# Gated expert rows scattered by token and choice, with the last norm in the experts' block, on one Trainium2 core

## What is computed

```python
gate_logits = x @ gate_w + gate_b
topk_vals, topk_idx = jax.lax.top_k(gate_logits, K)          # K = 2 of E = 16
topk_w = jax.nn.softmax(topk_vals, axis=-1)
h = jax.nn.relu(jnp.einsum('bsh,ehf->bsef', x, w1) + b1)     # 256 -> 512
expert_out = jnp.einsum('bsef,efh->bseh', h, w2) + b2        # 512 -> 256
sel = jnp.take_along_axis(expert_out, topk_idx[:, :, :, None], axis=2)
moe = jnp.sum(topk_w[..., None] * sel, axis=2)
y = x + moe
(y - mu) / jnp.sqrt(var + EPS) * gamma + beta                # and added to the residual
```

## Time and profile before

| | us |
|---|---|
| median of three runs | 1938.15 |
| the profiled execution | 1941.34 |
| its span, first to last instruction | 1939.4 |

### The profile page before, as it was taken

One profiled execution on the slowest core, in us unless ns is written; L12 is line 12 of the kernel. 1 busy time (PEld: TensorE's weight loads), 2 busy tenths in 40 slices (PEclk: granted clock), 3 DMA queues, 4 the chain that ended last, 5 costly groups with the idle time before them and its releaser, 6 DMA issues. The chain is left out here.

```text
span 1939.4 us, 33213 instructions
## 1 busy us (share of the span) xinstructions
PE 1445.2 (75%) x7648; PEld 1164.5 (60%) x7649; DVE 969.4 (50%) x3112; ACT 463.1 (24%) x1295; POOL 994.3 (51%) x1125
## 2 busy tenths in 40 slices
PE   5499968787769887877878788664899999996000
PEld 4366636565657665665756666442799899886000
DVE  8766556552737452742745275368211222221787
ACT  0144432121112111211212112010344444443000
POOL 0200027777777777777777777720233233223775
PEclk9799987989788899888899879775899999998555
DMA  6000043333333333333333333344322333532443
GB/s 215 1 0 0 0 144 104 104 106 103 103 105 104 103 103 105 103 104 105 103 103 105 105 101 105 104 132 137 113 78 70 113 94 95 189 92 64 131 137 115
DMA packets 105690, 193.84 MB, mean 100 GB/s; under 512 B 19056, under 2 KB 68976, under 8 KB 105520
## 3 DMA queue, kind: packets, MB, share of 16 engines
q0 software_dynamic: 47520, 129.82, 23.9%
q1 hardware_dynamic: 58128, 63.58, 9.8%
HBM read 159.11 MB, written 34.21 MB: 100 GB/s over the span
## 5 line engine op out<-in xcount | busy, mean ns | idle before, releaser
L701 POOL DMA_INDIRECT ring<-table,staged x784 | 747.5, 953 | 242.8 <-issue 226.3
L976 PE MATMUL bank<-ring,hots 128*128 x1372 | 323.9, 391 | 53.0 <-SPq L690 52.7
L976 PEld LDWEIGHTS bank<-ring,hots 128*128 128x128 f32 x1372 | 264.6, 195 | 102.7 <-issue 66.9
L1427 PEld LDWEIGHTS bank<-xT,w 128*128 128x128 f32 x1696 | 208.9, 194 | 15.5 <-issue 10.3
L1427 PE MATMUL bank<-xT,w 128*128 128x128 f32 x1696 | 210.2, 278 | 8.7 <-issue 8.7
L976 PE MATMUL bank<-ring,late_hots 128*128 x388 | 141.8, 518 | 97.4 <-SPq L690 88.8
L1405 ACT ACTIVATE hT<-bank,b 128x128 f32<-128x128 f32 x424 | 155.6, 367 | 226.0 <-PE bank L1427 202.4
L1435 PE MATMUL bank<-w,hT 128*128 128x256 f32 x848 | 201.7, 381 | 1.5 <-DVE y L1468 1.4
L786 DVE TENSOR_SCALAR hots<-iota_t,edge_l 128x128 f32<-128x128 f32 x686 | 182.1, 362 | 1.8
L976 PEld LDWEIGHTS bank<-ring,late_hots 128*128 128x128 f32 x388 | 92.5, 252 | 138.9 <-issue 124.3
L1348 POOL COPY at_x<-list 128x1 int32 (+1 forms) x108 | 19.6, 181 | 287.4 <-DVE xin L1450 201.2
(11 more groups left out here) (256 smaller groups left out, 2028.9 us busy)
## 6 DMA issues: line engine op xcount, KB each, us to landing
w<-in_w SPq DMA_DIRECT2D x32, 512.0 KB, 5.2
lists_out<-y SPq DMA_DIRECT2D x106, 128.0 KB, 2.7
ring<-table,staged POOLq DMA_INDIRECT x784
x<-in_x SPq DMA_DIRECT2D x1, 6272.0 KB, 23.4
table<-xn SPq DMA_DIRECT2D x7, 896.0 KB, 4.4
rows<-xn SPq DMA_DIRECT2D x1, 6272.0 KB, 21.1
out<-out_c SPq DMA_DIRECT2D x7, 512.0 KB, 3.1
out<-out_c SPq DMA_DIRECT2D x7, 384.0 KB, 2.6
```

The source lines that it names most:

```text
L701: pool.indirect_dma_start(out=ring[:, j, :], out_offset=None, in_=a.table, in_offset=bass.IndirectOffsetOnAxis(ap=staged[:, half, col:col ...
L976: last = nc.tensor.matmul(agg, hot[:, k, :], two[:, k, :], start=False, stop=False)
L1427: last = nc.tensor.matmul(up_ps[fc], w1[:, slot, ch, fc * P:(fc + 1) * P], xT[:, ch, :], start=(ch == 0), stop=(ch == DC - 1))
```

## The change

- **route**: the list gets a second column. The one-hot matmuls now carry `2 * lane + 1 + choice` instead of the lane, so that each list entry says token and choice. VectorE decodes it: which token to fetch, and in which row of the new HBM tensor `spread` (token, choice) the result belongs; unused rows go to dummy rows behind. `m.which` says per row which of the two gates applies. SyncE writes `rows` with 258 columns: the 256 of `m.xn` and the two gates, as two DMAs, the second after a wait on the gates.
- **experts**: GpSimd fetches rows of 258 columns and, itself, scatters each block's result to `spread` by an indirect DMA; SyncE sends no results and no zeros. VectorE, in iteration b, first waits for the result, adds the bias into a buffer of its own, waits for that and for a free half of `y`, copies the scatter's row numbers, multiplies by the gate into `y`; then it runs `rows_in(b + 2)`, which now also picks the gate out of the fetched rows and copies the row numbers of a later fetch, and only this last copy counts up `copied`. TensorE waits for `biased_ok` instead of `y_ok` before it reuses the result bank.
- **last norm**: in the same block. SyncE loads both rows of each token from `spread` by plain DMAs of four tiles, TensorE adds `m.xn` and the two rows in PSUM by three matmuls with the identity, and VectorE takes statistics and the norm from there, one batch of four tiles behind; ScalarE gives a seed by Ln and Exp.
- The buffers of the first stages are freed before the experts, and `with_beta` uses scalar_tensor_tensor.

```diff
@@ route
+        lane2 = sb("lane2", [P, 2], F16)
...
             sp.dma_start(rows[:, :, 0:D], m.xn[:]).then_inc(rows_out, 16)
+            sp.wait_ge(gates_ok, 1)
+            sp.dma_start(rows[:, :, D:D + 2], m.share[:]).then_inc(rows_out, 16)
             sp.dma_start(e.b1[:], a.b1).then_inc(e.b1_in, 16)
...
+            sp.wait_ge(rows_out, 32)
...
-                    dve.tensor_scalar(ids[part][:, :, 0], hi_hot[part][:], m.const[:, C_LANE:C_LANE + 1], None, ALU.mult)
+                    dve.tensor_tensor(ids[part][:, :, 0], hi_hot[part][:],
+                                      lane2[:, None, None, :].broadcast_to([P, n, BLOCKS, 2]), ALU.mult)
...
-            c.add(dve.tensor_tensor(m.list[:, 0:BLOCKS], tokens[:], list_ps[:, 0:BLOCKS], ALU.add))
+            c.add(dve.tensor_tensor(tokens[:], tokens[:], list_ps[:, 0:BLOCKS], ALU.add))
+            c.wait()
+            c.add(dve.tensor_copy(spot[:], tokens[:]))
+            c.add(dve.tensor_scalar(unused[:], tokens[:], 0.0, dummy[:, 0:1], ALU.is_equal, ALU.mult))
+            c.add(dve.tensor_copy(m.list[:, BLOCKS:BLOCKS + 1, 1], dummy[:]))
+            c.wait()
+            c.add(dve.tensor_single_scalar(first_i[:], spot[:], 1, ALU.bitwise_and))
+            c.add(dve.tensor_scalar(spot[:], spot[:], 1.0, -1.0, ALU.max, ALU.add))
+            c.wait()
+            c.add(dve.tensor_copy(m.which[:, 0:BLOCKS, 0], first_i[:]))
+            c.add(dve.tensor_scalar(m.which[:, 0:BLOCKS, 1], first_i[:], -1.0, 1.0, ALU.mult, ALU.add))
+            c.add(dve.tensor_single_scalar(spot[:], spot[:], 1, ALU.arith_shift_right))
+            c.wait()
+            c.add(dve.tensor_copy(m.list[:, 0:BLOCKS, 0], spot[:]))
+            c.add(dve.tensor_tensor(m.list[:, 0:BLOCKS, 1], tokens[:], unused[:], ALU.add))
@@ experts, GpSimd
+            def sent(of, n):
+                pool.wait_ge(y_ok, of + 2)
+                if not isinstance(of, int) or of > 0:
+                    pool.wait_ge(y_out, of * 16)
+                    pool.sem_inc(y_free, 1)
+                settle(pool, m)
+                pool.indirect_dma_start(out=a.spread, in_=y[:, 1 - n, :], in_offset=None,
+                                        out_offset=bass.IndirectOffsetOnAxis(ap=to[:, 1 - n:2 - n], axis=0)).then_inc(y_out, 16)
...
+                    fetched(i * 2 + (n + 4), n)
+                    landed(i + (n + 2), 1 - n)
+                    sent(i * 2 + (n + 1), n)
+            pool.wait_ge(y_out, pairs * 32 + 16)
+            pool.sem_inc(spread_ok, 1)
@@ experts, SyncE
+                    end = of_list(sp, 1, i * SLOTS + slot)
+                    sp.wait_ge(y_ok, end + 1)
+                    e.load(sp, i * SLOTS + (slot + SLOTS), slot)
+            sp.wait_ge(spread_ok, 1)
+            last_norm.sync(sp)
@@ experts, VectorE
             def rows_in(b):
                 dve.wait_ge(got_ok, b + 1)
                 if not isinstance(b, int) or b > 0:
                     dve.wait_ge(xtr_ok, b)
                     settle(dve, m)
-                dve.tensor_copy(xin[:], got[:, bass.ds(b % 2, 1), :].rearrange("p a d -> p (a d)")).then_inc(copied, 1)
+                dve.tensor_tensor(pick[:, bass.ds(b % 2, 1), :], got[:, bass.ds(b % 2, 1), D:D + 2], m.which[:, bass.ds(b, 1), :],
+                                  ALU.mult).then_inc(pick_ok, 1)
+                dve.tensor_copy(xin[:], got[:, bass.ds(b % 2, 1), 0:D].rearrange("p a d -> p (a d)"))
+                dve.wait_ge(pick_ok, b + 1)
+                settle(dve, m)
+                dve.tensor_tensor(gate[:, bass.ds(b % 4, 1)], pick[:, bass.ds(b % 2, 1), 0:1].rearrange("p a k -> p (a k)"),
+                                  pick[:, bass.ds(b % 2, 1), 1:2].rearrange("p a k -> p (a k)"), ALU.add)
+                fetched(b + 2)
...
                     with dve.Fori(first, end) as b:
+                        dve.wait_ge(down_ok, b + 1)
+                        dve.tensor_tensor(biased[:], down_ps, b2[:, slot, :], ALU.add).then_inc(biased_ok, 1)
+                        dve.wait_ge(biased_ok, b + 2)
+                        dve.wait_ge(y_free, b + 2)
+                        settle(dve, m)
+                        sent_to(b)
+                        dve.tensor_scalar(y[:, bass.ds(b % 2, 1), :].rearrange("p a d -> p (a d)"), biased[:], gate[:, bass.ds(b % 4, 1)],
+                                          None, ALU.mult).then_inc(y_ok, 1)
                         rows_in(b + 2)
-                        dve.wait_ge(down_ok, b + 1)
-                        dve.wait_ge(y_out, b * 16 + 16)
-                        dve.tensor_tensor(y[:], down_ps, b2[:, slot, :], ALU.add).then_inc(y_ok, 1)
@@ last norm, TensorE
+            if t >= 8:
+                pe.wait_ge(self.z_read, t - 8 + 1)
+            nc.tensor.matmul(to, m.ident, tile(m.xn, t), start=True, stop=False)
+            if t % 4 == 0:
+                pe.wait_ge(self.back[t // 4], 16)
+            for k in range(2):
+                last = nc.tensor.matmul(to, m.ident, self.got[:, t % self.LOADED, k, :], start=False, stop=(k == 1))
@@ last norm, VectorE
+        for q in range(len(self.batches)):
+            spreads(q)
+            if q > 0:
+                normal(q - 1)
+        normal(len(self.batches) - 1)
```

More of the change, by code:

```diff
@@ L32 @@
 BLOCKS = 2 * NP // BLOCK + E
-AHEAD = 2
 BATCH = 28
@@ L104, in memory @@
     m.places = sb("places", [P, NT, 2], I32)
[L105 removed]
+    m.list = sb("list", [P, BLOCKS + 4, 2], I32)
     m.lists = sb("lists", [1, 2, E], I32)
[L107 to L109 removed]
+    m.which = sb("which", [P, BLOCKS + 4, 2])
     m.ident = m.const[:, C_ID:C_ID + P]
@@ L1182, in _ @@
             c.wait()
-            c.add(dve.tensor_tensor(m.share[:, :, 1], eg[:], m.share[:, :, 0], ALU.mult))
+            dve.tensor_tensor(m.share[:, :, 1], eg[:], m.share[:, :, 0], ALU.mult).then_inc(gates_ok, 1)
             dve.wait_ge(rank_ok, 1)
@@ new lines, in _, with fetched @@
+            pool.sem_inc(y_free, 3)
+            pairs = nc.s_assert_within(of_list(pool, 1, E - 1) // 2, E // 2, BLOCKS // 2,
+                                       skip_runtime_bounds_check_because="half of all blocks")
+            def fetched(b, n):
+                pool.wait_ge(copied, b + 1)
+                settle(pool, m)
+                pool.indirect_dma_start(out=got[:, n, :], out_offset=None, in_=a.rows,
+                                        in_offset=bass.IndirectOffsetOnAxis(ap=at[:, n:n + 1], axis=0)).then_inc(x_in[n], 16)
@@ L1363, in _ @@
+            pool.wait_ge(x_in[1], pairs * 16 + 32)
+            settle(pool, m)
         @block.sync
         def _(sp):
-            def sent(i, more):
-                bounds = bounds_of(sp, i)
+            with sp.Fori(0, E // SLOTS - 1) as i:
                 for slot in range(SLOTS):
-                    first, end = bounds[slot:slot + 2]
-                    with sp.Fori(first, end) as b:
-                        sp.wait_ge(y_ok, b + 2)
-                        sp.dma_start(rows_of(a.lists_out, b), y[:]).then_inc(y_out, 16)
-                        sp.sem_inc(filled, 16)
-                    if more:
-                        e.load(sp, i * SLOTS + (slot + SLOTS), slot)
@@ L1577, in _ @@
[L1577 to L1591 removed]
+        self.m, self.a = m, a
@@ new lines, in __init__ @@
+        self.LOADED, self.DONE = 16, 12
+        self.batches = [(t, min(t + 4, NT)) for t in range(0, NT, 4)]
+        self.got = sb("got", [P, self.LOADED, 2, D])
+        self.z = sb("z", [P, 4, D])
+        self.out = sb("out_c", [P, self.DONE, D])
+        self.st = sb("st_c", [P, 2, 4, 6])
+        self.mv = sb("mv_c", [P, 2, 4, 2])
+        self.var = sb("var_c", [P, 2, 4])
+        self.lnv = sb("lnv_c", [P, 2, 4])
+        self.seed = sb("seed_c", [P, 2, 4])
+        self.nt = sb("nt_c", [P, 4])
```

321 lines of the change are left out of this document (153 added, 168 removed).

## The result

The changed kernel takes 2003.6 us (median of 4 runs, 2003.14 to 2004.04) against 1938.63 us: a ratio of 1.034, 95% interval 1.032 to 1.036. It is slower, as forecast, but by 65 us where 32 were forecast; the executions of each kernel agree within 0.3%.

| stretch | before | after | difference | forecast |
|---|---|---|---|---|
| up to the first product of the experts | 1369.65 | 1371.91 | +2.3 | +3 |
| from there to the last bias add | 409.6 | 519.3 | +109.7 | +69 |
| last bias add to the end | 160.1 | 109.7 | -50.4 | -40 |

The account below looks back on a forecast made before the run. TensorE was taken to bound the experts' loop, while the last stretch, with TensorE idle, could be shortened. Route +3, loop +69 and end -40 gave +32, so 1970 us, with an 8 in 10 range of 1918 to 2030.

Parts of the forecast that it names:

- The part named as the one that counts: Experts' loop: VectorE's work from the bias add to `copied` outlasts the 1.37 us TensorE leaves; +69 us.
- Route: Route: lane product as tensor_tensor, some seven more dependent steps, small memsets and copies, all on VectorE; +3 us.
- The gate pieces: Route: SyncE's 6272 writes of 8 bytes, priced from nothing to 21.1 us, costed at nothing for the first product.
- I take 0.65 us, nearer to the middle: Experts' loop: the TensorE stall chosen per block, with register instructions partly under work; 106 blocks, +69 us.
- middle case: Experts' loop: register instructions run beside the work in front; chain 1.82 us, stall 0.45 us a block, 48 us.
- upper case: Experts' loop: thirteen register instructions and five waits, none hidden after the bias; chain 2.54 us, stall 1.17, 124 us.
- lower case: Experts' loop: register instructions cost nothing, wait behind the bias 0.19; chain 1.63 us, stall about 0.28 a block, 30 us.
- The second term, the last stretch: Last bias add to the end: first norm at 28 us, cycles of 8.0, 120.6 us against 160.1; -40 us.
- a clock of 0.9: Last norm: TensorE's assumed granted clock, which makes the cycle of four tiles 8.0 us instead of 7.4.
- The hidden stall: Rival, experts' loop: reordering nearly hidden, stall 0.28 us a block, last norm at full clock; 1925 us, chance 0.30.
- Half clock in the last norm: Rival, last norm: TensorE's pauses keep it at 1.2 GHz, cycle 13 us; 2020 us, chance 0.12.
- GpSimd as the pace: Rival, experts' loop: fetch and scatter wait for each other's landing, 5.1 us a block; 2049 us, chance 0.07.

Follow-up runs that it names:

- order alone: Kernel before with only the order changed: VectorE waits for the result and adds the bias, then takes in the rows of block b + 2; 1944.95 us, ratio 1.0019.
- `xin` behind the bias: Changed kernel with the copy to `xin` right behind the bias add and its own count for TensorE; 1898.79 us, ratio 0.978.
- the two edits of its stream: GpSimd waits for a fetch's landing right behind it, before the scatter, in the changed kernel with rows taken first or `xin` right behind the bias; ratios 1.053 and 1.058.
- my first experiment: Changed kernel, but VectorE takes in the rows of block b + 2 before it waits for the result of block b; 1977.16 us, ratio 1.0186.

## Why the prediction was right in kind and wrong in size

**What held.** The part named as the one that counts was the one: the rows moved behind the result, with 1.37 us of room, and a longer chain. Experiments at four lengths of that chain agree: 0.75 us (order alone, and `xin` behind the bias; both periods 3.73), 2.06 to the end of `xin` (4.31) and 2.56 to `at` (4.82). Route cost 2.3 us for my 3. GpSimd's two indirect DMAs, the weight loads and the beta additions cost nothing visible in that order. The gate pieces stayed hidden, as priced: they landed 21.7 us after their issue, the weights behind them were issued from 1326.9 on instead of 1309.6, and the first product came 2.3 us later, no more than the 2.9 that route itself took longer.

**The term that was mis-sized: "I take 0.65 us, nearer to the middle".** The stall was 1.09 us in a block in the middle of the loop, and the loop grew by 109.7 us for my 69. The step that failed is the middle case's "these run beside the work in front", taken to mean that a register instruction adds nothing beyond its own 0.12. The starts in the block above, against those of the middle case:

| from start to start | middle case | measured |
|---|---|---|
| bias add to `to` | 0.77 | 0.87 |
| `to` to `y` | 0.12 | 0.21 |
| `y` to `pick` | 0.29 | 0.56 |
| `pick` to `xin` | 0.12 | 0.13 |
| `xin` to `gate` | 0.23 | 0.36 |
| `gate` to `at` | 0.12 | 0.28 |
| `at` to its end | 0.17 | 0.15 |
| sum | 1.82 | 2.56 |

The register instructions do start beside the work in front: in this block the first one behind an operation begins 0.02 us after that operation has started (a semaphore instruction behind `xin` 0.08). But one of 0.14 us with the gaps around it takes longer than a small operation shows, so that `y` and `at` start 0.21 and 0.28 after theirs and not 0.12. In front of `pick` it is a register instruction for a wait, a semaphore instruction and two address instructions of 0.16 and 0.09, which do not fit under the 0.35 of `y`. VectorE's wait for its own result was 0.44, with the longer register instruction of `to`, for my 0.35 from the earlier trace rows. The order-alone run shows the other side: one register instruction under 0.42 of work is free.

That the upper case's 2.54 meets the measured 2.56 is luck. Its thirteen instructions of 0.12 and five of 0.04 are 1.76 us, which on top of the 1.63 of the lower case would be 3.39 and not 2.54. (A smaller slip: the lower case's 1.63 less 1.37 is 0.26, not 0.28.) Between the end of the bias add and the start of `at` the stream held seven fused register instructions (0.05 to 0.16 us), three plain ones and three semaphore instructions, 1.11 us in all, and a part of that ran under work. And a chain of 2.56 less the room of 1.37 would be a stall of 1.19; it was 1.09, since from the turning to the next bias add the changed kernel takes 4.83 - 2.62 = 2.21 us, where it was 3.73 - 1.37 = 2.36.

**The second term, the last stretch: -50.4 for my -40.** Its beginning came out at 27.8 us to the first norm, 28 forecast, by two errors that cancel: the first rows were there after 13.8 us and not 13, the eight tiles took 13.0 and not 14. The cycle was 6.97 us and not 8.0, and that is the whole difference: ten cycles, 10 us. Of the 1.03 us a cycle, 0.6 are what I had added for a clock of 0.9, where the clock was 1.00 in all ten batches. The rest is the price of a matmul and of what follows: 0.53 to the first read, 5.48 for four tiles and 0.96 for the last statistics, where I had 0.5, 5.7 and 1.2. I had priced a matmul by 1.89/4 = 0.47, where the profile models the end of the group; in the changed kernel a tile's first matmul follows the last tile's after 1.29 us, 0.43 a matmul:

```profile
1915.29 0.59 PE L1594 MATMUL bank<-xn,const 128*128 128x256 f32 x2
...
1916.58 0.59 PE L1594 MATMUL bank<-xn,const 128*128 128x256 f32 x2
```

The gain at the end was 10 us larger than forecast, the loss in the loop 41 larger; that is the +61.5 between the spans for the +32 of the sum.

**The rivals.** The hidden stall (0.30) is out by the chain's 2.56 us. Half clock in the last norm (0.12) is out: 1.00 over the ten batches, with TensorE busy 78% (54.48 of 70 us) and pausing 1.53 us in each. The page TensorE: Matmul & The Clock Gate of the Trainium skill (A second HAM failure mode: psum-queue depth-cycling) says of a kernel in bf16 with N = 512 that its small idle gaps, while it cycles through PSUM banks, make the clock fall and rise again. This trace, in float32 with 256 columns, does not show that: eight banks are cycled, with a pause in each batch, and the clock stays at 1.00 from 1919 to 1989. The lower mean of 0.93 comes from the half clock after the pause at the end of the experts. The clock did fall in the version with one matmul a tile, to 0.57 with TensorE busy 55% (32.09 of 58.1 us), so the rival was not far off: with a third of the matmuls it came about. GpSimd as the pace (0.07) is not so in the changed kernel, but the two edits of its stream made it so, and with the rows first it is part of the ring that the trace shows. I had checked GpSimd's order only for the order of the changed kernel; that is why my first experiment was expected at 1890 and came at 1977.

## What to carry to other kernels

When an operation is moved behind a result that another engine waits for in turn, count the whole stream up to the instruction that tells that engine, from start to start and with the register and semaphore instructions between (0.21 to 0.28 us behind a small operation here, for operations that last 0.15), and compare it with the room in the timeline. Then count up the semaphore at the instruction the other engine needs, and put that instruction first: here that alone turned 3.4% slower into 2.2% faster, with the same work. And before an order is turned round, follow each wait through every engine's stream: a message that stands behind unrelated work in a relay engine closes a ring that no busy time shows.

## What the runs showed of the hardware that was not expected

- A copy of one column at positions held in registers lengthened the block by 0.13 us, at fixed positions by 0.03, though each copy lasts about 0.15 us by its record: what counts is the distance between starts.
- TensorE's clock stayed at 1.00 over 70 us with 78% busy and a pause of 1.53 us every 6.97 us, and was 0.57 over 58 us in the version where it was busy 55%.
- 6272 pieces of 8 bytes landed 21.7 us after their issue at 1309.6, about the 21.1 of as many pieces of 1 KB. This is no price of theirs alone, since the write of `rows` was still under way: issued at 1295.0, it landed after 28.5 us instead of 21.1, with rows of 1032 bytes instead of 1024 and the small write behind it. The two causes were not told apart.
- The kernel before took 16% to 20% longer on two other chips. The changed kernel's trace on the third chip has all of the extra time before route. There GpSimd's gathers waited 268.6 us for TensorE in 70 waits, and the DMA queues moved 79 GB/s where the first chip's moved 103; the cause was not looked for.
